# Rounding by ScalarE in place and one subtraction on GpSimd, with squares in four column tiles, roots sent by ScalarE and reciprocals by token halves

## The reference

```python
Bm = rmsnorm((x @ WB.T).reshape(B_, L, H, N), Bn_w) + B_bias     # the same for Cm
dt = softplus(x @ Wdt.T);  theta = (x @ Wth.T).reshape(B_, L, H, N // 2)
theta_cumsum = cumsum(theta * dt[..., None], axis=1)
Bm = rope(Bm, theta_cumsum);  Cm = rope(Cm, theta_cumsum)        # cos and sin of the running angle
# per token: h = alpha * h + beta * outer(B_prev, x_prev) + gamma * outer(B, x);  y = C . h
y = y * silu(z);  out = y @ Wout.T
```

## Time and profile before

| | |
|---|---|
| median of three runs | 3594.47 us (3583.92 to 3598.4) |
| the profiled execution's own time | 3601.3 us |
| its span | 3599.5 us |
| mean granted PE clock | 0.88 of full speed |
| busy share PE, DVE, ACT, POOL | 81%, 66%, 51%, 43% |

### The profile page before, as it was taken

How to read it: one execution, slowest core, us unless ns; L and a number is a source line. 1 busy time by engine, 2 the same in 40 slices (tenths; PEclk the granted TensorE clock), 3 DMA queues, 4 the chain that set the end, 5 groups by cost and what they waited for, 6 DMA issues and landing times.

```text
span 3599.5 us, 84310 instructions
## 1 busy us (share of the span) xinstructions
PE 2897.9 (81%) x28752; PEld 2199.6 (61%) x28752; DVE 2374.4 (66%) x3926; ACT 1820.9 (51%) x3740; POOL 1539.4 (43%) x1420
## 2 busy tenths in 40 slices
PE   5139957788888899999977999999899998279573
PEld 4128846466666657667654667676676676168462
DVE  5214224699999849889945988884888885243135
ACT  1016624566666356666614666663666672046331
POOL 3550050255555416655610555551455553510345
PEclk7559968889899899999978999998999998589785
DMA  9537755466665246556403666642666653467564
GB/s 387 197 123 254 255 163 179 142 183 184 177 184 176 77 139 171 164 162 171 134 3 119 173 172 172 171 134 68 170 172 171 172 160 115 158 206 254 175 205 138
DMA packets 311258, 605.54 MB, mean 168 GB/s; under 512 B 59136, under 2 KB 159616, under 8 KB 310016
## 3 DMA queue, kind: packets, MB, share of 16 engines
q1 hardware_dynamic: 286464, 535.63, 48.9%
q0 software_dynamic: 24576, 67.14, 5.6%
HBM read 446.25 MB, written 155.32 MB: 167 GB/s over the span
## 4 chain that ended last, share of the span: by engine, by line
PE 53%; DVE 19%; issue 10%; another core or an unknown queue 7%; ACT 4%; DMA 4%; POOL 1%; DVEq 1%; SPq 1%; POOLq 0%; ACTq 0%
PE bank L63 15%; PE bank L568 7%; PE bank L1327 4%; DVE tmp L1275 3%; PE bank L1197 3%; PE bank L1393 3%; DVE xbc L1251 3%; DMA rc_in<-decay_t 3%; PE bank L581 2%; PE bank L559 2%; PE bank L1391 2%; PE cs_sn L581 2%; PE bank L1367 2%; DVE rot L1275 2%
## 5 line engine op out<-in xcount | busy, mean ns | idle before, releaser
L63 PE MATMUL bank<-xh,wb 128*128 128x512 f32 x2048 | 685.4, 416 | 73.1 <-ACT btr L1342 43.2
L644 DVE TENSOR_TENSOR hh<-sg,bank 128x96 f32<-128x96 f32 x384 | 97.5, 254 | 596.4 <-ACT sg L619 372.6
L63 PEld LDWEIGHTS bank<-xh,wb 128*128 128x128 f32 x2048 | 373.3, 192 | 190.4 <-ACT btr L1342 63.9
L1206 ACT ACTIVATE xbc<-bank,norm_w 128x512 f32<-128x512 f32 x512 | 350.7, 685 | 240.8 <-PE bank L63 234.1
L1295 POOL TENSOR_TENSOR sq<-cst,rho 128x512 f32<-128x512 f32 x128 | 133.5, 1043 | 742.8 <-DVE xbc L1251 411.3
L1283 POOL TENSOR_TENSOR rot<-rot,tmp 128x512 f32<-128x512 f32 x256 | 341.8, 1335 | 238.3 <-DVE tmp L1275 238.3
L568 PE MATMUL bank<-wgu,xgT 128*128 (+1 forms) x1536 | 343.7, 350 | 107.6 <-issue 68.2
L63 PE MATMUL bank<-xl,wb 128*128 128x512 f32 x1024 | 408.5, 399 | 0.0
L1284 POOL TENSOR_TENSOR rot<-rot,tmp 128x512 f32<-128x512 f32 x256 | 358.7, 1401 | 0.0
L568 PEld LDWEIGHTS bank<-wgu,xgT 128*128 128x128 f32 x1536 | 261.0, 204 | 118.5 <-issue 118.1
L1275 DVE SCALAR_TENSOR_TENSOR rot<-xbc,bias,cs_sn 128x1024 f32<-128x1024 f32 x256 | 325.4, 1271 | 8.4 <-DVE xbc L1251 6.8
(11 more groups left out here) (277 smaller groups left out, 6084.7 us busy)
## 6 DMA issues: line engine op xcount, KB each, us to landing
wb<-watt_dram SPq DMA_DIRECT2D x96, 1024.0 KB, 7.7
rr_bc<-rr_dram SPq DMA_DIRECT2D x128, 512.0 KB
yd<-ys SPq DMA_DIRECT2D x96, 512.0 KB
wd<-w_down SPq DMA_DIRECT2D x384, 96.0 KB
watt_dram<-wb SPq DMA_DIRECT2D x32, 1024.0 KB, 5.4
dt_bc<-row_dram SPq DMA_DIRECT2D x256, 128.0 KB
al_bc<-row_dram SPq DMA_DIRECT2D x256, 128.0 KB, 3.2
xd<-xg SPq DMA_DIRECT2D x12, 2048.0 KB, 23.7
```

The source lines that it names most:

```text
L63: ins = e.matmul(dst, a, m, start=start and c == 0, stop=stop and c == n - 1, skip_group_check=not (start and stop))
L1206: e.activation(xbc[j % 4][:, i, :], of(i)[:, :], ACT.Copy, scale=norm_w[:, i:i + 1])
```

## The change

It has six parts.

1. **Rounding.** `T_act2` writes cum + MAGIC into `nfr` (SBUF) and takes MAGIC off again in place with a second ACT instruction; one subtraction on POOL, `T_pool2`, behind `own_pool`, makes `nfr`. `T_dve2` is gone from DVE. `T_pe` waits only for `cum`, and `Y_dve` has a buffer of its own.
2. **Squares.** `ss_pe` computes token halves: 8 matmuls of 256 columns in four column tiles, instead of 4 of 512 columns in two.
3. **Roots.** `R_act` reads 100x256 instead of 36x512, and stands ahead of `T_act2` instead of behind it.
4. **Sending the roots.** `R_sp1` becomes `R_rows_act`: two DMAs, one for each token half, issued by ACT behind `T_act2`. The reciprocals and `rr_bc` are laid out by token halves.
5. **Transposes.** The first `tr_pe` goes ahead of `G_pe`, and waits for the B half of `F_pool` alone.
6. **Scan 0.** `wb_low_dve` and `th_low_dve` move from behind `F_dve3` to ahead of `K_dve1` of the next turn, the ACT parts of the split behind the last `A_act`, and SP's stores and loads of these weights behind the loads of rows.

```diff
         def T_act2(e, m, j):
             e.wait_ge(e_cum.sem, e_cum.at(m + 1))
             e.wait_ge(e_nfr.sem, e_nfr.at(m))
-            e.activation(W[2][:, :], cum[:, :], ACT.Identity, bias=magic[:, 0:1]).then_inc(e_rnd.sem, 1)
+            e.wait_ge(e_cs.sem, e_cs.at(m))
+            e.activation(nfr[:, :], cum[:, :], ACT.Identity, bias=magic[:, 0:1]).then_inc(e_rs.sem, 1)
+            e.wait_ge(e_rs.sem, e_rs.at(m + 1))
+            e.activation(nfr[:, :], nfr[:, :], ACT.Identity, bias=minus_magic[:, 0:1]).then_inc(e_rnd.sem, 1)
...
-        def T_dve2(e, m, j):
+        def T_pool2(e, m, j):
             e.wait_ge(e_rnd.sem, e_rnd.at(m + 1))
-            e.wait_ge(e_cs.sem, e_cs.at(m))
+            e.nop(nofuse=True)
             e.wait_ge(e_cum.sem, e_cum.at(m + 1))
-            e.scalar_tensor_tensor(nfr[:, :], W[2][:, :], MAGIC, cum[:, :], ALU.subtract, ALU.subtract).then_inc(e_nfr.sem, 1)
+            e.tensor_tensor(nfr[:, :], nfr[:, :], cum[:, :], ALU.subtract).then_inc(e_nfr.sem, 1)
...
             for eo in range(2):
-                for ty in range(2):
-                    first = 30 - 28 * (1 - ty) - 2 * (j % 2)
-                    ins = e.matmul(SSB[32 * ty:32 * ty + 32, :], one_hot[:, first:first + 32], sq4[:, 2 * ty + eo, :],
-                                   start=j % 2 == 0 and eo == 0, stop=j % 2 == 1 and eo == 1, skip_group_check=True)
+                for half in range(2):
+                    for ty in range(2):
+                        first = 30 - 28 * (1 - ty) - 2 * (j % 2)
+                        g = 64 * half + 32 * ty
+                        ins = e.matmul(SSB[g:g + 32, 0:HALF], one_hot[:, first:first + 32], sq4[:, 2 * ty + eo, half * HALF:(half + 1) * HALF],
+                                       start=j % 2 == 0 and eo == 0, stop=j % 2 == 1 and eo == 1, skip_group_check=True)
...
-            e.activation(stdr, SSB[0:36, :], ACT.Sqrt, scale=1.0 / NS, bias=eps_nm[0:36, 0:1]).then_inc(e_sr.sem, 1)
+            e.activation(stdr, SSB[0:100, 0:HALF], ACT.Sqrt, scale=1.0 / NS, bias=eps_nm[0:100, 0:1]).then_inc(e_sr.sem, 1)
...
-        def R_sp1(e, gm):
+        def R_rows_act(e, gm):
...
-            e.dma_start(rc_in[:, :], stdr[NORM_ROWS, :].rearrange("r (c w) -> r c w", w=32)).then_inc(a_r1.sem, 16)
+            for h in range(2):
+                e.dma_start(rc_in[CL * h:CL * h + CL, :], stdr[NORM_ROWS[h], :].rearrange("r (c w) -> r c w", w=32)).then_inc(a_r1.sem, 16)
```

More of the change, by code:

```diff
@@ L173, in build @@
         end_bc = [sb(f"end_bc{i}", [P, ENDW]) for i in range(4)]
-        rr_bc = [sb(f"rr_bc{i}", [P, 4, SEQ]) for i in range(2)]
+        rr_bc = [sb(f"rr_bc{i}", [P, 2, 4, SEQ // 2]) for i in range(2)]
         wb, th = ([sb(f"{n}{i}", [P, 2, w], F32R) for i in range(2)] for n, w in (("wb", BCW), ("th", THW)))
@@ L212, in build @@
         row_dram = nc.dram_tensor("row_dram", [NP, 2, ROWW], F32, kind="Internal").ap()
-        rr_dram = [nc.dram_tensor(f"rr_dram{i}", [8, SEQ], F32, kind="Internal").ap() for i in range(2)]
+        rr_dram = [nc.dram_tensor(f"rr_dram{i}", [16, SEQ // 2], F32, kind="Internal").ap() for i in range(2)]
         a_const, a_x = arr("a_const"), arr("a_x")
@@ L1469, in turn_act @@
                     T_act3(e, n, j)
+                if RG:
+                    R_act(e, gm + 1)
                 if T:
@@ L1472, in turn_act @@
                 if RG:
[L1473 removed]
+                    R_rows_act(e, gm + 1)
                 if K:
@@ L1523, in turn_dve @@
                 F_dve2(e, n, j, b * (NP // 2) + it * 2 + j // 2 + 1)
-                if T:
-                    T_dve2(e, n + 1, j + 1)
+                if is_first(b) and not (first and j == 0) and not (last and j >= 1):
+                    wb_low_dve(e, q + 3, j + 1)
+                if is_first(b) and not (first and j == 0) and not (last and j >= 2):
+                    th_low_dve(e, q + 2, j)
                 if K:
@@ L1536, in turn_dve @@
                     gather_turn_dve(e, b, n, q, it, j)
-                if is_first(b) and not last:
-                    wb_low_dve(e, q + 4, j)
-                if is_first(b) and not (last and j >= 1):
-                    th_low_dve(e, q + 3, j + 1)
                 if K:
@@ L1550, in turn_sp @@
                 gm = b * (NP // 2) + it * 2 + j // 2
-                if is_first(b) and not (last and j >= 1):
-                    wb_store_sp(e, q + 3, j + 1)
-                if is_first(b) and not last:
-                    wb_load_sp(e, b, q + 4, j)
-                if is_first(b) and not (last and j >= 2):
-                    th_store_sp(e, q + 2, j)
                 if not (last and j >= 2):
@@ L1563, in turn_sp @@
                     end_sp(e, q + 2, j + 2)
+                if is_first(b) and not (last and j >= 1):
+                    wb_store_sp(e, q + 3, j + 1)
+                if is_first(b) and not last:
+                    wb_load_sp(e, b, q + 4, j)
+                if is_first(b) and not (last and j >= 2):
+                    th_store_sp(e, q + 2, j)
                 if not (last and j >= 1):
```

53 lines of the change are left out of this document (28 added, 25 removed).

## The result

The changed kernel takes 3608.27 us (median of 17 runs, 3596.09 to 3621.17), the kernel before 3600.24 in the same runs. The ratio is 1.0026 [1.0014, 1.0037]: 0.3% slower, where I had forecast 3.5% faster. The profiled execution took 3613.62 us, its span is 3611.6.

What follows compares the result with a forecast made beforehand. DVE was taken to bound scan 0, a ring through DVE, PE and ACT scans 1 to 3. Gains of 81 us (scans 1 to 3) and 48 us (scan 0), 129 off 3601.3, gave 3472; predicted 3470, range 3425 to 3530.

Steps and rivals of the forecast that it cites:

- Landing: Roots' DMA in scans 1 to 3: sent from ACT, they land 4.2 us after issue; bounds 3.3 and 6.3.
- The roots don't pass the `wb` load: Rival: roots land after 5.8 to 6.3 us, DVE's ring 0.9 to 1.4 us longer; 3520 us, 15%.
- that ring: Ring through the landing: `K_dve2` ends 8.7 us behind the projections' start, PE wants it at 9.4; 0.7 us spare.
- the three signs of being wrong: DVE waits over 1 us a group for roots; ACT's issues over 1 us each; POOL's rope sums start later.
- Nothing comes of it: Rival: subtraction pushes `F_pool` back in many turns, products and `K_dve1` give PE's gain back; about 3590 us, 5%.
- It costs nothing: POOL's added subtraction, 1.29 us, hides in its 1.9 us a turn of idle time; uncovered, up to 1.3 us.
- Squares: Sums of squares on PE: 0.95 us a turn instead of 1.91, as four column tiles overlap.
- Issues: ACT issues the roots' two DMAs at 0.45 us each, 0.9 us together, ahead of both `K_act` copies.
- Rounding: ACT's rounding takes 0.63 + 0.07 + 0.63 us instead of 0.69, +0.64 a turn; DVE loses 0.68 us.
- I cost that at nothing: Transposes ahead of `G_pe`: products come 0.55 us later, covered by DVE's 3.4 us of gaps a group.
- Scan 0: DVE-bound: lost subtraction and cheaper splits bring a group from 35.6 to 32.4 us; gain 48 us.
- The ring that is left: Ring on ACT and PE in scans 1 to 3: 28.4 us a group, taken as 28.5 for all three.

Runs made afterwards that it cites:

- e2: Changed kernel with the odd turn's `wb` load in scans 1 to 3 issued by SP behind the roots instead of ahead: 3542.72 us, ratio 0.9834.
- e1: Changed kernel with the roots' two transfers issued by SP again, at their old place: 3643.39 us, ratio 1.0111.
- e10: e6 with part 1 undone (DVE subtracts again, ACT rounds once, POOL subtracts nothing): 3533.49 us, ratio 0.9787.
- e6: e2 with POOL's index copy and indirect DMA (scatters) of scans 2 and 3 moved behind `D_pool`: 3517.95 us, ratio 0.9733.
- e5: e2 with the products ahead of the first transposes again, as before the change: 3538.64 us, ratio 0.9822.
- e14: e6 with the products ahead of the first transposes again in all four scans: 3517.36 us, ratio 0.9751.
- e7: Kernel before with part 6 alone added: 3629.48 us, ratio 1.0045.
- e11: e6 with part 6 undone: 3605.97 us, ratio 0.9998.
- the two corrections: Odd turn's `wb` load behind the roots, and scatters of scans 2 and 3 behind `D_pool`; on the changed kernel this is e6: 3517.95 us, ratio 0.9733.

## Why the prediction was wrong

- **The step that failed is "Landing".** "From ACT they need not stand in SP's queue" took a place in SP's program for the place in the DMA engines. The roots landed 6.3 us after the first issue in the group shown and 6.5 to 7.0 at the median of scans 1 to 3, not 4.2; with the load behind them (e2) it is 3.1 to 3.8, and from SP again (e1) 6.4 to 6.9. The rival "The roots don't pass the `wb` load" had the mechanism right, at 15%. It had priced it at 1.1 us a group for a landing of 5.8 to 6.3; e2 gives 1.5 to 1.8 in scans 2 and 3. By the forecast's own sum for that ring, a landing of 6.5 to 6.8 is 1.6 to 1.9 us too late, so the price was short because the landing was. In scan 1 e2 gives 0.5, with four bouts of program loads in it.
- **The row behind the 4.2 us.** The row that I had taken as the nearest, `al_bc` at 3.3 us, stood behind the `wb` load too, only later: the issues behind that median come 4.5 us after the load's, which lands after 7.9, so 3.3 us was the rest of the same queue. After the change, issued 1.5 us behind the load, `al_bc` takes 5.9 us at the median.
- **The signs.** Of the three signs of being wrong the first came: DVE waits 24.4/14 = 1.7 us a group for the roots. ACT's issues took 0.62 us, and POOL's wait for DVE's rope products fell from 52.7 to 28.2 us. The rival nearest in time, "Nothing comes of it" at 3590, named another mechanism. DVE's wait for the products did grow, but e2 leaves the order of transposes and products as it is and gains 1.9%.
- **POOL's cover.** "It costs nothing" held for the subtraction, 1.29 us in the idle time: part 1 undone (e10) gives back 0.2 us a group in scans 2 and 3. Not seen at all was that POOL's indirect DMA can hold back PE's updates: 16 of 64 turns before. Moving that DMA was worth 1.0% in e6, not all of it by the late updates.
- **Program length.** I priced the four extra calls of the sums of squares by PE time alone. They save nearly what I said, but with the change PE's loop reloads its program in some passes of scan 1, in eleven of fifteen profiles, and without it in none of four. That these calls do it is likely and not shown.
- **Squares**: 1.07 us a turn against 0.95; four tiles overlap. **Root** 0.47 against 0.45. **Issues** 0.62 us each against 0.45. **Rounding**: from the start of the first to the end of the second 1.46 us against 1.33. One by one ACT's terms are 0.5 us too low, and yet their sum came out, 3.9 to 4.1 us from the end of the sines to the end of the second issue against 1.75 + 1.33 + 0.9 = 3.98. I had put the issues behind the rounding, and the first runs beside its last 0.54 us: two errors that cancel, so luck.
- **Transposes first.** "I cost that at nothing" was wrong in scan 1, where the part loses 0.6 us a group (e5 against the level groups of e6). In scans 2 and 3 it gains, but 0.3 us (e14), where I had taken 0.94 off the ring.
- **Scan 0** came out as forecast, 31.9 against 32.4, and splits at 2.7 us against 2.9. But I had added its terms as if each stood alone; e7 and e11 show that part 6 costs 1.4 us a group in the kernel before and is worth 5.7 beside the other parts. The hit is in part luck.
- **The ring that is left**: with the two corrections it is 28.2 us in scans 2 and 3 where I had 28.4 to 28.5. That is in part luck too, since the second correction was not in the forecast, and with clean landings alone it is 29.5 to 29.8. From the changed kernel to e2 it is 69 us by the ratios, from e2 to e6 36, and the last 28 us to the forecast are scan 1's: 31.1 us a group instead of 28.5.
